# Attention with exact maxima, then expert layers: the row maxima are split and sent in two halves of heads

## The reference

```python
q, k, v = (split(q), split(k), split(v))
scores = jnp.einsum('...hqd,...hkd->...hqk', q, k) / np.sqrt(DH)
scores = jnp.where(causal, jnp.float32(-1000000000.0), scores)
weights = jax.nn.softmax(scores, axis=-1)
out = jnp.einsum('...hqk,...hkd->...hqd', weights, v)
```

## Time and profile before

| what | value |
| --- | --- |
| median of 3 runs | 620.13 us (618.73 to 623.44) |
| the profiled execution | 618.61 us |
| its span in the profile | 616.5 us (2.1 us lie around it) |
| prologue, to the first copy of the maxima | about 43 us |
| bodies 0 to 15 and tail | 43 to 303 us |
| expert layers | 303 to 616.5 us |
| TensorE busy over the span | 84% |
| VectorE, ScalarE, GpSimd busy | 74%, 59%, 55% |

### The profile page before, as it was taken

How to read it: one execution, slowest core, us unless ns; L and a number is a source line. 1 busy time by engine, 2 the same in 40 slices (tenths; PEclk the granted TensorE clock), 3 DMA queues, 4 the chain that set the end, 5 groups by cost and what they waited for, 6 DMA issues and landing times.

```text
span 616.5 us, 15252 instructions
## 1 busy us (share of the span) xinstructions
PE 516.2 (84%) x4916; PEld 441.4 (72%) x4931; DVE 458.3 (74%) x1295; ACT 363.5 (59%) x984; POOL 339.1 (55%) x459
## 2 busy tenths in 40 slices
PE   3169999999889988897499999998996664879995
PEld 2137667677667766674389999998995553779995
DVE  5565777977998799767398796554998887887662
ACT  2114566866576657464266776665776755656663
POOL 2104444444456664566776777777863844465555
PEclk9766999999999999897789999999998766799998
DMA  6663444444454453416442433222783212545320
GB/s 159 128 134 85 108 116 105 106 105 107 104 109 117 125 122 79 112 32 232 147 103 60 108 97 91 83 82 80 214 305 100 80 53 86 142 158 144 97 69 17
DMA packets 59531, 69.44 MB, mean 113 GB/s; under 512 B 9241, under 2 KB 50657, under 8 KB 57148
## 3 DMA queue, kind: packets, MB, share of 16 engines
q1 hardware_dynamic: 51744, 53.01, 33.7%
q0 software_dynamic: 7168, 14.77, 7.2%
q10 hardware_dynamic: 540, 0.69, 0.6%
HBM read 45.31 MB, written 23.67 MB: 112 GB/s over the span
## 4 chain that ended last, share of the span: by engine, by line
PE 31%; DVE 6%; issue 3%; ACT 3%; DMA 3%; POOL 2%; SPq 2%; DVEq 1%; POOLq 0%; ACTq 0%
PE h_ps_e L1868 13%; PE y_ps_e L1880 13%; PE xT_ps_e L1856 2%; DMA xt_e<-expert_queues 1%; POOL expert_rows L1287 1%; DVE x L1497 1%; PE h_ps_e L1937 1%; ACT hT_e L1712 1%; POOL expert_queues L1139 1%; DVE xn_e L1526 1%; SPq L1367 1%; DVEq L1418 1%; ACT L1727 1%; ACT rxr L1774 1%; DVE stats L1501 1%
## 5 line engine op out<-in xcount | busy, mean ns | idle before, releaser
L624 DVE TENSOR_REDUCE mx<-max_ps 128x2 f32<-128x512 f32 (+1 forms) x192 | 127.0, 687 | 48.7 <-PE max_ps L277 47.0
L1712 ACT ACTIVATE hT_e<-h_ps_e,wb_e 128x128 f32<-128x128 f32 x448 | 121.9, 389 | 26.2 <-PE h_ps_e L1868 25.4
L1868 PE MATMUL h_ps_e<-xT_e,wb_e 128*128 128x128 f32 x896 | 113.3, 281 | 2.4 <-ACT hT_e L1712 1.0
L1880 PE MATMUL y_ps_e<-wb_e,hT_e 128*128 128x128 f32 x896 | 109.3, 275 | 2.8 <-DVE yt_e L1437 2.8
L1868 PEld LDWEIGHTS h_ps_e<-xT_e,wb_e 128*128 128x128 f32 x896 | 107.8, 196 | 4.3 <-issue 2.3
L1880 PEld LDWEIGHTS y_ps_e<-wb_e,hT_e 128*128 128x128 f32 x896 | 104.5, 192 | 3.1 <-DVE yt_e L1437 3.0
L462 ACT ACTIVATE pT<-sc_ps 128x1024 f32<-128x1024 f32 x64 | 65.5, 1023 | 55.6 <-PE sc_ps L305 55.5
L1287 POOL DMA_INDIRECT expert_rows<-yt_e,go_e x72 | 78.7, 1093 | 29.5 <-issue 17.9
L1424 DVE COPY wb_e<-wpack 128x1156 f32 x112 | 83.5, 787 | 8.9 <-issue 5.1
L870 POOL TENSOR_TENSOR turn<-eps 128x1 f32<-128x1 f32 x64 | 13.0, 203 | 138.8 <-ACT pT L462 138.8
L58 POOL DMA_INDIRECT expert_queues<-rxr,rseats x64 | 66.2, 1034 | 19.6 <-issue 16.9
(11 more groups left out here) (286 smaller groups left out, 974.3 us busy)
## 6 DMA issues: line engine op xcount, KB each, us to landing
wpack<-in_wpack SPq DMA_DIRECT2D x2, 4112.0 KB, 14.9
parts_scratch<-parts SPq DMA_DIRECT2D x16, 384.0 KB, 3.0
xt_e<-expert_queues SPq DMA_DIRECT2D x40, 129.0 KB
xt_e<-expert_queues SPq DMA_DIRECT2D x72, 64.5 KB
wpack<-parts_scratch SPq DMA_DIRECT2D x24, 192.0 KB
kst<-parts_scratch SPq DMA_DIRECT2D x24, 192.0 KB
qst<-parts_scratch SPq DMA_DIRECT2D x72, 64.0 KB
wpack<-parts_scratch SPq DMA_DIRECT2D x63, 64.0 KB
```

What stands on the lines that cost most here:

```text
L624: nc.vector.reduce_max(mx[:, s, h0:h0 + n], max_ps[:, (k + 1) % 2, :].rearrange("p (h k) -> p h k", h=n), axis=AX.X).then_inc(unit_reduced, 1)
L1712: last = nc.scalar.activation(hT[i % 2][:, s, c, :], h_ps[h_bank(i)][:, s, c * RT:(c + 1) * RT], ACT.Relu, bias=wb[i % 4][:, s, FF + c:FF ...
L1868: last = nc.tensor.matmul(h_ps[h_bank(i)][:, s, c * RT:(c + 1) * RT], wb[i % 4][:, s, c * P:(c + 1) * P], xT[i % 2][:, s * RT:(s + 1) * RT ...
L1880: last = nc.tensor.matmul(y_ps[i % 2][:, s * D:(s + 1) * D], hT[i % 2][:, s, c, :], wb[i % 4][:, s, FF + FC + c * D:FF + FC + (c + 1) * D] ...
```

## The change

The heads are cut in two halves of eight, with a buffer `mpad`, `mT` and semaphores for each.

- Units are renumbered: units 0 and 1 take the first token tile of heads 0 to 7, 2 to 5 the second tile of the same heads, and 6 to 11 the same for heads 8 to 15. After unit 5 the first half's maxima are complete.
- GpSimd splits the first half (`split_first`, five instructions of 128 x 16, each waiting for the one before), between `drop_future` 1 and 2 of the body before.
- TensorE transposes it into bank 1 of `mix_ps` between values 1 and scores 3, and ScalarE copies it between the exponentials 2 and 3. SyncE sends its rows behind the store.
- VectorE splits the second half where it split everything before, with four instructions of 128 x 16, and its transposes, copy and rows stand where the old ones stood.
- Scores 0 wait for the first half's rows, scores 2 for the second half's. The stack load waits for the second half's rows, as it waited for all before.
- In the prologue VectorE splits both halves, one behind the other.

```diff
         mx = sb("mx", [P, TPS, H], F32)
-        mres = sb("mres", [P, TPS, H], F32)
-        mpad = sb("mpad", [P, TPS, P], BF16)
-        mparts = mpad[:, :, 0:NPART * H].rearrange("p s (a h) -> p s a h", h=H)
-        mT = sb("mT", [NPART * H, S], BF16)
+        HH = H // 2
+        mneg, mres = (sb(n, [P, TPS, HH], F32) for n in ("mneg", "mres"))
+        mpad = [sb(f"mpad{i}", [P, TPS, P], BF16) for i in range(2)]
+        mparts = [m[:, :, 0:NPART * HH].rearrange("p s (a h) -> p s a h", h=HH) for m in mpad]
+        mT = [sb(f"mT{i}", [NPART * HH, S], BF16) for i in range(2)]
         pT = [sb(f"pT{u}", [P, 3 * 512], F32) for u in range(NQ)]
...
         unit_done, unit_reduced = sem("unit_done"), sem("unit_reduced")
-        msplit, mparts_ready = sem("msplit"), sem("mparts_ready")
-        mT_done, mT_ready, mrows_loaded = sem("mT_done"), sem("mT_ready"), sem("mrows_loaded")
+        first_split = sem("first_split")
+        msplit = [sem(f"msplit{i}") for i in range(2)]
+        mparts_ready, mT_done, mT_ready, mrows_loaded = ([sem(f"{n}{i}") for i in range(2)] for n in ("mparts_ready", "mT_done", "mT_ready", "mrows_loaded"))
         v_done, v_ready = sem("v_done"), sem("v_ready")
...
-            return (0, 4 * k, 4) if k < 4 else (1, 2 * (k - 4), 2)
+            h, j = k // 6, k % 6
+            return (0, 8 * h + 4 * j, 4) if j < 2 else (1, 8 * h + 2 * (j - 2), 2)
...
             if counts(shifted):
-                eng.wait_ge(mrows_loaded, shifted * 16)
+                eng.wait_ge(mrows_loaded[1], shifted * 16)
             if counts(read):
...
                 pe.wait_ge(resid_ready, projected)
+                if counts(c):
+                    pe.wait_ge(mT_ready[0], c + 1)
                 if counts(normed):
...
                 if k == 1 and counts(c):
-                    pe.wait_ge(mT_ready, c)
+                    pe.wait_ge(mT_ready[1], c)
                 if counts(c * NU + k - 1):
...
-            def transpose_max(c):
-                pe.wait_ge(mparts_ready, c + 1)
-                out = max_ps[:, 0, :].bitcast(BF16)
+            def transpose_max(c, h):
+                pe.wait_ge(mparts_ready[h], c + 1)
+                if not h:
+                    pe.wait_ge(resid_ready, min(c + LEAD, NSEQ))
+                    if c == 0:
+                        pe.wait_ge(v_ready, 2)
+                out = (max_ps if h else mix_ps)[:, 1 - h, :].bitcast(BF16)
                 for s in range(TPS):
-                    last = nc.tensor.transpose(out[:, s * P:(s + 1) * P], mpad[:, s, :], identb[:])
-                last.then_inc(mT_done, 1)
+                    last = nc.tensor.transpose(out[:, s * P:(s + 1) * P], mpad[h][:, s, :], identb[:])
+                last.then_inc(mT_done[h], 1)
...
                     pe.wait_ge(stack_loaded[r], transfers(c, r, NB, LD))
-                    pe.wait_ge(mrows_loaded, (c + 1) * 16)
+                    pe.wait_ge(mrows_loaded[0], (c + 1) * 16)
                     if c == 0:
                         pe.wait_ge(ones_loaded, 16 * NB)
+                if u == 2:
+                    pe.wait_ge(mrows_loaded[1], (c + 1) * 16)
                 for bk in range(3):
...
                     unit(0, 0, k)
-                transpose_max(0)
+                transpose_max(0, 0)
+                transpose_max(0, 1)
...
                 if s4:
-                    transpose_max(b)
+                    transpose_max(b, 1)
                 next_units(0, 1)
...
                 values(b, r, 1)
+                if s2:
+                    transpose_max(b + 1, 0)
                 scores(b, r, 3)
...
-            def copy_mT(c, r):
-                act.wait_ge(mT_done, c + 1)
+            def copy_mT(c, h):
+                act.wait_ge(mT_done[h], c + 1)
                 if counts(c * 16):
-                    act.wait_ge(mrows_loaded, c * 16)
-                nc.scalar.copy(mT[:], max_ps[:, 0, :].bitcast(BF16)[0:NPART * H, 0:S]).then_inc(mT_ready, 1)
+                    act.wait_ge(mrows_loaded[h], c * 16)
+                nc.scalar.copy(mT[h][:], (max_ps if h else mix_ps)[:, 1 - h, :].bitcast(BF16)[0:NPART * HH, 0:S]).then_inc(mT_ready[h], 1)
...
                 exp(b, 2)
+                if s2:
+                    copy_mT(b + 1, 0)
                 exp(b, 3)
...
                     take_v(b + 1, (r + 1) % NB)
-                    copy_mT(b + 1, (r + 1) % NB)
+                    copy_mT(b + 1, 1)
...
                 dve.wait_ge(unit_done, c * NU + k + 1)
-                if k == 0:
-                    if counts(3 * c):
-                        dve.wait_ge(msplit, 3 * c)
-                    if counts(c):
-                        dve.wait_ge(mparts_ready, c)
+                if k % 6 == 0 and counts(c):
+                    dve.wait_ge(mparts_ready[k // 6], c)
                 s, h0, n = unit_heads(k)
...
-            def split_max(c):
-
-                dve.wait_ge(unit_reduced, NU * (c + 1))
+            def split_max(c, h):
+
+                m = mx[:, :, h * HH:(h + 1) * HH]
+                dve.wait_ge(unit_reduced, NU * c + 6 * (h + 1))
                 if counts(c):
-                    dve.wait_ge(mT_done, c)
-                nc.vector.tensor_scalar(mparts[:, :, 0, :], mx[:], -1.0, None, ALU.mult).then_inc(msplit, 1)
-                dve.wait_ge(msplit, 3 * c + 1)
-                nc.vector.scalar_tensor_tensor(out=mres[:], in0=mx[:], scalar=-1.0, in1=mparts[:, :, 0, :],
-                                               op0=ALU.mult, op1=ALU.subtract).then_inc(msplit, 1)
-                dve.wait_ge(msplit, 3 * c + 2)
-                nc.vector.tensor_copy(mparts[:, :, 1, :], mres[:]).then_inc(msplit, 1)
-                dve.wait_ge(msplit, 3 * c + 3)
-                nc.vector.tensor_tensor(mparts[:, :, 2, :], mres[:], mparts[:, :, 1, :], ALU.subtract).then_inc(mparts_ready, 1)
+                    dve.wait_ge(mT_done[h], c)
+                if not h and counts(c):
+                    dve.wait_ge(mparts_ready[1], c)
+                if h:
+                    dve.wait_ge(mparts_ready[0], c + 1)
+                nc.vector.tensor_scalar(mparts[h][:, :, 0, :], m, -1.0, None, ALU.mult).then_inc(msplit[h], 1)
+                dve.wait_ge(msplit[h], 3 * c + 1)
+                nc.vector.scalar_tensor_tensor(out=mres[:], in0=m, scalar=-1.0, in1=mparts[h][:, :, 0, :],
+                                               op0=ALU.mult, op1=ALU.subtract).then_inc(msplit[h], 1)
+                dve.wait_ge(msplit[h], 3 * c + 2)
+                nc.vector.tensor_copy(mparts[h][:, :, 1, :], mres[:]).then_inc(msplit[h], 1)
+                dve.wait_ge(msplit[h], 3 * c + 3)
+                nc.vector.tensor_tensor(mparts[h][:, :, 2, :], mres[:], mparts[h][:, :, 1, :], ALU.subtract).then_inc(mparts_ready[h], 1)
...
                     reduce_unit(0, k)
-                split_max(0)
+                split_max(0, 0)
+                split_max(0, 1)
...
                 if s2:
-                    split_max(b + 1)
+                    split_max(b + 1, 1)
                 if at == "B":
...
                                         ALU.subtract).then_inc(parts_ready, 1)
+
+            def split_first(c):
+
+                m = mx[:, :, 0:HH]
+                pool.wait_ge(unit_reduced, NU * c + 6)
+                pool.wait_ge(mT_done[0], c)
+                nc.gpsimd.tensor_scalar(mneg[:], m, -1.0, None, ALU.mult).then_inc(first_split, 1)
+                pool.wait_ge(first_split, 4 * c - 3)
+                nc.gpsimd.tensor_copy(mparts[0][:, :, 0, :], mneg[:]).then_inc(first_split, 1)
+                pool.wait_ge(first_split, 4 * c - 2)
+                nc.gpsimd.tensor_tensor(mneg[:], mneg[:], mparts[0][:, :, 0, :], ALU.subtract).then_inc(first_split, 1)
+                pool.wait_ge(first_split, 4 * c - 1)
+                nc.gpsimd.tensor_copy(mparts[0][:, :, 1, :], mneg[:]).then_inc(first_split, 1)
+                pool.wait_ge(first_split, 4 * c)
+                nc.gpsimd.tensor_tensor(mparts[0][:, :, 2, :], mneg[:], mparts[0][:, :, 1, :], ALU.subtract).then_inc(mparts_ready[0], 1)
...
                 drop_future(b, 1)
+                if s2:
+                    split_first(b + 1)
                 if at == "D" and g:
...
-            def load_rows(c, r):
+            def load_rows(c, r, h):
                 ready = value(sp, c + 1)
-                sp.wait_ge(mT_ready, ready)
-                sp.dma_start(qst[r][KS:KM, :, :], mT[:]).then_inc(mrows_loaded, 16)
+                sp.wait_ge(mT_ready[h], ready)
+                sp.dma_start(qst[r][KS:KM, h * HH:(h + 1) * HH, :], mT[h][:]).then_inc(mrows_loaded[h], 16)
...
                     sp.dma_start(t[name][:], dram[name].to_broadcast([P, E])).then_inc(consts_loaded, 16)
-                load_rows(0, 0)
+                load_rows(0, 0, 0)
+                load_rows(0, 0, 1)
                 load_stack(2, 2)
...
                 if s2:
-                    load_rows(b + 1, (r + 1) % NB)
+                    load_rows(b + 1, (r + 1) % NB, 0)
```

(1 more changed line is left out.)

4 lines of the change are left out of this document (3 added, 1 removed).

## The result

The changed kernel takes 617.7 us (median of 16 runs, 613.7 to 620.9) beside 621.4 us for the kernel before in the same comparison (16 runs): a ratio of 0.9947, 95% interval 0.9924 to 0.9970. It is faster by 0.5%, some 3.3 us (the medians lie 3.7 us apart). The forecast was slower by 0.6% (3.8 us). "Within 1%" held, the range of 617 to 630 just held the time, and the sign was wrong.

What follows compares the result with a forecast made beforehand. TensorE was taken to bound most bodies, VectorE bodies 7, 8, 11 and 12. Terms 8.7 + 1.0 + 0.5 - 4.9 - 1.5 = +3.8 us on a median of 620.1 gave 623.9 us, range 617 to 630.

Steps and rivals of the forecast that it cites:

- Within 1%: Whole kernel: time differs by less than 1% (6.2 us) from the kernel before; chance 0.63.
- the wait before the transposes: TensorE before scores 3: waits 0.77 us per body for GpSimd's split, in nine bodies bound by TensorE.
- the new order: Renumbered units: heavier units moved to places 6 and 7 cost TensorE 0.11 us in nine bodies, 1.0 us.
- A and D bodies are unchanged: Bodies 7, 8, 11 and 12, bound by VectorE: existing TensorE waits cover the new wait, so no change.
- cover: TensorE's waits for VectorE, up to 1.5 us (reductions, A bodies) and 1.1 us (choice, D bodies), absorb the new wait.
- the hold: GpSimd's split: VectorE's 0.43 us cast beside it holds a GpSimd operation, adding 0.35 us.
- the lead: Between GpSimd's end of mask 1 and TensorE reaching scores 3: 1.11 us available for the split.
- the term of 8.7 us: Wait for GpSimd plus 0.20 us of transposes, 0.97 us per body, paid in nine bodies bound by TensorE.
- The removed row wait: TensorE's wait before scores 0, 6.7 us in ten times, goes; 4.9 us gained in bodies bound by TensorE.
- The last body: Its 1.47 us wait before the first scores goes, making the end 1.5 us earlier.
- the quick chain: Rival: GpSimd's split takes 1.1 us, TensorE's wait 0.1, giving 617.4 us; chance 0.24.
- The stack loads take over: Rival: q and k stack loads come late in shorter bodies; no gain beyond 1 or 2 us, 620; chance 0.04.

Runs made afterwards that it cites:

- run 2: Kernel before with only the new numbering of the units: 619.4 us, 0.9956 of the kernel before.
- the idle operations (3): Kernel before plus five dependent GpSimd operations of the split's shapes, on buffers nobody uses: 622.6 us, 0.9988 of the kernel before.
- the explicit wait (9): Kernel before, with GpSimd's third part of a residual waiting for VectorE's row scalings in A bodies: 618.8 us, 0.9968 of the kernel before.
- run 6: Changed kernel with the first half's transposes behind scores 3 and ScalarE's copy behind its last exponential: 614.8 us, 0.9927 of the kernel before.
- run 1: Changed kernel with scores 0 made to wait for the rows of both halves: 621.4 us, 0.9994 of the kernel before.
- run 10: Changed kernel with later transposes and earlier stack loads, ScalarE's copy again ahead of its last exponential: 613.8 us, 0.9876 of the kernel before.
- one changed index: Changed kernel with stack loads of q and k sent after the first half's rows, not the second's: 615.4 us, 0.9929 of the kernel before.

## Why the prediction was wrong

Its steps, forecast against the two profiled executions, from one end of attention to the other:

```
                               forecast   measured
prologue and body 0              +0.5       +2.1
light bodies 2-6, 9, 10, 13, 14  +4.8       +1.8
body 1                            0         +0.2
A bodies 8 and 12                 0         -3.4  (about -1.6 without before's clock stretch)
D bodies 7 and 11                 0         -0.3  (-2.1 in the second profile after)
last body                        -1.5       -2.6
sum                              +3.8       -2.3
```

Two steps failed: what VectorE does in the A and D bodies was missing from the sum, and the wait before the transposes was priced at twice its size. With the wait and the transposes as measured, and the new order at its measured 1.9 us, the sum would be +0.6 us; the A and D bodies and a larger gain in the last one take it below zero.

**The step that failed in its mechanism is "A and D bodies are unchanged"**, the "cover". I took TensorE's wait for VectorE as a cushion that could only swallow cost, and never asked what made VectorE late. The row of body 8 in the earlier trace rows had the question in it: 16.31 us of VectorE work in a body where others have 11.4 to 11.8. I did not read the durations of the scalings, 336 ns at least and 1197 at most for the same shape. GpSimd's third part held them, and each of three edits that move it against them gives 0.9 to 1.5 us in body 8: the order of the units (2), the idle operations (3), the explicit wait (9). None has the early rows. In the D bodies the choice of experts was held in the same way, and the 1.1 us that TensorE waited for it, my other cover, went to nothing in body 7 and to 0.5 in body 11. There the trace alone shows it; no run moved the third part in D bodies by itself.

**The wait before the transposes** was a mis-sized term, and the largest error by size: 0.39 us instead of 0.77, over nine bodies 3.5 instead of 6.9 us. The split was 0.15 us shorter than forecast (gaps 0.29 instead of 0.40, the hold 0.27 instead of 0.35, the operations 1.09 instead of 1.05); the lead was wrong by 0.18, of which 0.11 is the priced unit that was not credited with giving GpSimd time. The transposes were 0.12 instead of 0.20 us, so the term of 8.7 us was 4.6. Against it, the new order, charged with 1.0 us, cost 1.9 in the same bodies by run 2. That the wait is lost time run 6 shows: without it the median is lower by 3.2 us.

**The removed row wait** went as forecast, though not for nothing: 0.21 us of idle time now stands at line 279 of each light body for VectorE's reduction, and run 1, which has the row wait again, loses only 1.75 us in the nine bodies where 4.9 had been put. The terms do not simply add: run 1 has less row wait than the kernel before, 4.5 instead of 6.7 us. Of the light bodies' +1.8 us, half is body 4, an A body that I had counted as light (15.02 to 15.89 us).

**The last body** gained 2.4 to 2.6 us, not 1.5. In the nine profiles of kernels that need only the first half's rows at scores 0 it lasts 18.9 to 19.9 us, in the five of kernels that wait there for all rows (before, 1 to 3, 9) 21.3 to 22.2. The scores start at 1.38 us instead of 3.02 after the copy, which is 1.64; for the rest TensorE's clock may stand (0.73 before, in the earlier trace rows, 0.78 after over the same 21.6 to 21.9 us). With the same early rows it lasts 19.93 us at 0.74 (run 10) and 18.9 to 19.4 at 0.82 to 0.87 (the other eight). I did not test that part.

**The prologue** came out 1.6 us dearer than forecast, but there profiles of kernels with the same prologue differ by 3.5 us (body 1 starts at 61.6 to 65.1 us with the changed one, at 60.0 to 62.6 with the old one). How much of the 2.1 is the change stays open.

**Among the rivals** the quick chain gave the right time (617.4), and by the prediction's own sign, a wait under 0.4 us at line 294, it was this one (0.39). But it wanted a wait of 0.34 and a split of 1.37 us or less to come out even, and 0.1 and 1.1 us for 617.4; the split took 1.65. That its time came out is luck: with the measured wait and transposes the same sum gives -0.3 us, and the rest came from bodies that it had as unchanged. "The stack loads take over" was true in part in the D bodies: the load behind the second half's rows hid their gain, 1.2 us of wait in body 7 in the one profile and 0.4 in the other.

## What to carry to other kernels

Where an engine bounds a body, look at the durations of its own operations, minimum beside median and maximum, before treating its time as fixed: a held operation is waiting time that the page counts as work, and a shift of some tenths of a microsecond elsewhere can release it. When an edit delays one engine and another engine's operation stands in that delay, credit the delay with the cover that it gives as well as charging it. After a wait is removed, look for loads that are started by the event which has stayed where it was; here one changed index was worth 2.5 us by the medians, beside 3.3 us for the whole change, though 0.4 to 1.9 us by the bodies of the profiles.
